# A Mamba and mixture-of-experts layer on one core: new order of its head, new places for its last two chunks

## What is computed

```python
h = _layernorm(x) * (1 + ca) + sa
u = conv1d_depthwise(h, conv_w, taps=4) + conv_b
x_dbl = u @ xproj_w.T                       # dt (128), B (16), C (16)
delta = softplus(dt @ dtproj_w.T + dtproj_b)
h_t = exp(delta * A) * h_{t-1} + delta * B * u      # 16 states per channel
y = sum_n(h * C) + u * D_skip
x = x + ga * y
h = _layernorm(x) * (1 + cb) + sb
logits = tanh(h @ Wg1.T) @ Wg2.T; scores = softmax of the top 2 of 8
x = x + gb * sum_e(scores_e * (silu(h @ Wup_e.T + bup_e) @ Wdown_e.T + bdown_e))
```

## Time and profile before

| | |
|---|---|
| median of three runs | 1440.03 us |
| profiled execution | 1442.15 us |
| its span | 1440.4 us |
| PE busy | 1337.2 us (93%), 7512 instructions |
| DVE busy | 1258.5 us (87%) |
| POOL busy | 1140.5 us (79%) |
| ACT busy | 985.7 us (68%) |
| mean granted PE clock | 0.971 |
| DMA | 160.91 MB, mean 112 GB/s |

### The profile page before, as it was taken

The page is one execution under the profiler, slowest core; times in us unless marked ns, Lnnn a source line. Parts: engine busy times, 40 slices in busy tenths (PEclk is TensorE's granted clock), DMA queues, the critical chain, the costliest instruction groups (busy, mean ns, idle before and its releaser), DMA issues. The chain is left out here.

```text
span 1440.4 us, 23450 instructions
## 1 busy us (share of the span) xinstructions
PE 1337.2 (93%) x7512; PEld 964.4 (67%) x7512; DVE 1258.5 (87%) x1782; ACT 985.7 (68%) x2056; POOL 1140.5 (79%) x1157
## 2 busy tenths in 40 slices
PE   8788768999999999999999999999999999979898
PEld 4456545667766775667667776677676666667687
DVE  4799999899998999899988999899979999795475
ACT  3875786578848785579748885679758765655464
POOL 1699889699997989798988999798979888752243
PEclk9899877999999999999999999999999999999999
DMA  5441112235342434434333424243343343322342
GB/s 196 168 148 60 59 37 87 97 98 157 111 126 78 158 95 117 126 111 130 111 118 100 165 87 137 85 147 118 102 129 93 118 117 117 95 78 70 105 128 91
DMA packets 99250, 160.91 MB, mean 112 GB/s; under 512 B 9245, under 2 KB 33949, under 8 KB 99129
## 3 DMA queue, kind: packets, MB, share of 16 engines
q1 hardware_dynamic: 99128, 159.42, 35.8%
HBM read 150.60 MB, written 8.79 MB: 111 GB/s over the span
## 5 line engine op out<-in xcount | busy, mean ns | idle before, releaser
L785 POOL TENSOR_TENSOR DB<-DU,BR 128x512 f32<-128x512 f32 x448 | 575.6, 1299 | 44.7 <-DVE DU L1177 22.2
L1218 DVE SCALAR_TENSOR_TENSOR ACC<-pb,CTM,ACC 128x512 f32<-128x512 f32 x512 | 374.4, 731 | 52.0 <-PE pb L1419 51.7
L983 ACT ACTIVATE pb<-DELP,AN 128x512 f32<-128x512 f32 x448 | 307.3, 687 | 142.1 <-DVE H L1193 141.4
L1498 PE MATMUL pb<-WD,G 128*128 128x512 f32 x832 | 393.6, 593 | 0.0
L1419 PEld LDWEIGHTS pb<-ID,H 128*128 128x128 f32 x2048 | 245.8, 144 | 157.6 <-issue 89.9
L1419 PE MATMUL pb<-ID,H 128*128 128x128 f32 x2048 | 317.4, 281 | 34.2 <-DVE ACC L1218 29.2
L808 POOL TENSOR_TENSOR G<-TY 128x256 f32<-128x256 f32 x256 | 199.5, 780 | 182.1 <-DVE TY L1274 136.3
L1468 PE MATMUL pb<-H2H,WUH 128*128 128x256 f32 x1024 | 316.6, 309 | 23.0 <-DVE TY L1274 23.0
L1193 DVE TENSOR_TENSOR_SCAN H<-pb,DB 128x512 f32<-128x512 f32 x256 | 309.5, 1210 | 15.1 <-ACT pb L983 13.0
L1470 PE MATMUL pb<-H2H,WUL 128*128 128x256 f32 x1024 | 292.1, 285 | 0.0
L1469 PE MATMUL pb<-H2L,WUH 128*128 128x256 f32 x1024 | 291.8, 285 | 0.0
(11 more groups left out here) (200 smaller groups left out, 1739.4 us busy)
## 6 DMA issues: line engine op xcount, KB each, us to landing
WD<-in_wdT SPq DMA_DIRECT2D x128, 512.0 KB, 5.0
BR<-bscr SPq DMA_DIRECT2D x112, 256.0 KB, 3.9
SR<-sscr SPq DMA_DIRECT2D x128, 128.0 KB, 4.4
DU<-in_x SPq DMA_DIRECT2D x8, 1024.0 KB, 6.7
ACC<-in_x SPq DMA_DIRECT2D x16, 512.0 KB, 3.9
out<-ACC SPq DMA_DIRECT2D x32, 256.0 KB, 2.1
BR<-bscr SPq DMA_DIRECT2D x32, 128.0 KB, 3.3
DU<-in_xpT SPq DMA_DIRECT2D x8, 320.0 KB, 3.2
```

The lines of the kernel that those rows point to most:

```text
L785: eng.tensor_tensor(DB[:, i % NDB], DU[:, c % 2, r], BR[:, n % 2], ALU.mult).then_inc(S["dbu"], 1)
L983: eng.activation(DA[i % NDA][:], DEL[:, c % 2, r], ACT.Exp, scale=AN[:, r, n:n + 1]).then_inc(S["da"], 1)
L1218: eng.scalar_tensor_tensor(out=acc, in0=banks[bank_of["flip", c, n, r]][:], scalar=1.0 if n < 0 else CTM[:, c % 2, j, st:st + 1], in1=acc, ...
L1498: eng.matmul(DN[j][:], G[:, (cs * NM + m) % NG, j * 128:j * 128 + 128], WD[:, (cs * NE + m // 2) % NWD, m % 2], start=False, stop=m == NM ...
```

## The change

In the head: the tap order goes tile by tile (three taps of tile 0, then of tile 1, with tiles 2 and 3 mixed); `decay` moves behind the taps; `diag` moves from the place just after the first scan to ahead of the statistics, and now waits for its own inputs; `gbcp` moves behind the first `da`; the weights of row group 0 are loaded in two halves with a semaphore each, and the product waits for the second half in its middle. In chunk 1's table the statistics (`sta`, `nma`, `stb`) get later places. For chunks 6 and 7 the tables FAST, TAIL, FAST_PAIRS, TAIL_PAIRS, LOW and three of ROUTER get new numbers, and the split of the down products starts at pair (13,3) and not (13,0). The diff, cut:

```diff
 ATTENTION1 = {
-    "ldx": -11, "sta": (2, 2, 7, 8), "nma": 6, "stb": (11, 11, 14, 22), "rsa": 23, "pad": 36,
+    "ldx": -11, "sta": (5, 6, 8, 10), "nma": 11, "stb": (12, 12, 15, 22), "rsa": 23, "pad": 36,
...
-HEAD_TAPS = ((0, 2), (0, 1), (1, 2), (0, 0), (2, 2), (1, 1), (3, 2), (2, 1), (1, 0), (3, 1), (2, 0), (3, 0))
+HEAD_TAPS = ((0, 2), (0, 1), (0, 0), (1, 2), (1, 1), (1, 0), (2, 2), (2, 1), (3, 2), (2, 0), (3, 1), (3, 0))
...
-TAIL = {"sr": -1, "wd": 1, "up": (-3, -2), "th": (4, 4), "ys": (7, 7), "t1": (4, 7), "g": (7, 7), "dn": (16, 16),
-        "to": (18, 18), "fin": (16, 25), "out": (20, 34), "gbl": 17, "xa": 34}
+TAIL = {"sr": -9, "wd": -11, "up": (-2, -1), "th": (3, 3), "ys": (6, 7), "t1": (4, 5), "g": (7, 7), "dn": (1, 14),
+        "to": (16, 19), "fin": (18, 21), "out": (12, 29), "gbl": -4, "xa": 37}
...
-FAST_PAIRS = [51, 58, 64, 72, 77, 82, 86, 96, 101, 108, 112, 117, 122, 127, 133, 138]
-TAIL_PAIRS = [69, 74, 86, 91, 118, 126, 130, 135, 143, 149, 157, 166, 169, 179, 186, 196]
+FAST_PAIRS = [51, 58, 64, 70, 76, 82, 87, 92, 99, 106, 111, 116, 123, 131, 142, 156]
+TAIL_PAIRS = [71, 85, 100, 109, 120, 134, 138, 144, 150, 156, 165, 180, 185, 195, 202, 211]
...
-SPLIT_FROM = (13, 0)
-LOW = {"wh": (5, 5), "wl": 11, "gh": (7, 8), "gl": (11, 12), "dn": (14, 16)}
+SPLIT_FROM = (13, 3)
+LOW = {"wh": (5, 5), "wl": 8, "gh": (9, 10), "gl": (9, 12), "dn": (18, 18)}
...
-FIRST = ((1, ("diag",)), (4, ("gbt",)), (4, ("gbm",)), (8, ("gbb",)), (10, ("gbe",)), (11, ("rowz", 4)),
+FIRST = ((4, ("gbt",)), (4, ("gbm",)), (8, ("gbb",)), (10, ("gbe",)), (11, ("rowz", 4)),
...
-    a = [("begin",), ("warm", -1, WARM["begin"])] + [("sta", 0, j) for j in range(4)] + [("rsa", 0)] + [("xn", 0, j) for j in range(4)]
-    a += [("pad", 0), ("decay",), ("rows", 1), ("rcp", 1), ("rows", 0), ("rcp", 0), ("tr", 0, 0), ("rt", 1), ("mod", 1)]
+    a = [("begin",), ("warm", -1, WARM["begin"]), ("diag",)] + [("sta", 0, j) for j in range(4)] + [("rsa", 0)] + [("xn", 0, j) for j in range(4)]
+    a += [("pad", 0), ("rows", 1), ("rcp", 1), ("rows", 0), ("rcp", 0), ("tr", 0, 0), ("rt", 1), ("mod", 1)]
...
-    a += [("warm", -2, WARM["proj"])]
+    a += [("decay",), ("warm", -2, WARM["proj"])]
...
-                    eng.dma_start(WM[0], wm_v[0]).then_inc(S["d_wm0"], 16)
+                    eng.dma_start(WM[0][:, 0:2], wm_v[0][:, 0:2]).then_inc(S["d_wm0"], 16)
+                    eng.dma_start(WM[0][:, 2:4], wm_v[0][:, 2:4]).then_inc(S["d_wmh"], 16)
...
                     for kk in range(4 if what == "rows" else 1):
+                        if g == 0 and kk == 2:
+                            eng.wait_ge(S["d_wmh"], 16)
```

More of the change, by code:

```diff
@@ L71 @@
              "r52": 104, "sw": 104},
-    "final": {"fst": (17, 18), "nmf": 20, "fsu": (22, 22), "frs": 23, "fxn": (35, 37), "ftr": (44, 49),
-             "fev": (47, 49), "hh": 58, "hl": (59, 71), "r1": 79, "r12": 81, "r2": 85, "r22": 88, "r3": 91,
-             "r31": 93, "e1": 94, "r4": 93, "r40": 95, "r41": 95, "r42": 96, "sel1": 95, "sel2": 97, "r5": 96,
-             "r52": 101, "sw": 101},
-    "last": {"fst": (16, 19), "nmf": 27, "fsu": (25, 25), "frs": 27, "fxn": (35, 39), "ftr": (46, 49),
-             "fev": (47, 50), "hh": 52, "hl": (52, 58), "r1": 54, "r12": 56, "r2": 60, "r22": 60, "r3": 64,
-             "r31": 64, "e1": 64, "r4": 67, "r40": 67, "r41": 69, "r42": 72, "sel1": 70, "sel2": 73, "r5": 77,
-             "r52": 76, "sw": 77},
@@ L80 @@
-    "split": {"fst": (-43, -39), "nmf": -42, "fsu": (-39, -39), "frs": -38, "fxn": (-35, -33), "ftr": (-35, -29),
-             "fev": (-31, -27), "hh": -25, "hl": (-25, -24), "r1": -26, "r12": -20, "r2": -20, "r22": -20, "r3": -19,
-             "r31": -18, "e1": -17, "r4": -18, "r40": -15, "r41": -15, "r42": -15, "sel1": -14, "sel2": -12,
-             "r5": -11, "r52": -10, "sw": -4}}
+    "final": {"fst": (17, 22), "nmf": 26, "fsu": (24, 24), "frs": 26, "fxn": (36, 38), "ftr": (43, 45),
+             "fev": (46, 49), "hh": 58, "hl": (57, 70), "r1": 81, "r12": 86, "r2": 89, "r22": 84, "r3": 96,
+             "r31": 96, "e1": 97, "r4": 98, "r40": 100, "r41": 100, "r42": 100, "sel1": 103, "sel2": 103, "r5": 107,
+             "r52": 106, "sw": 106},
@@ new lines @@
+    "last": {"fst": (14, 19), "nmf": 27, "fsu": (25, 25), "frs": 31, "fxn": (36, 43), "ftr": (46, 51),
+             "fev": (47, 50), "hh": 55, "hl": (52, 60), "r1": 55, "r12": 56, "r2": 60, "r22": 61, "r3": 66,
+             "r31": 66, "e1": 67, "r4": 69, "r40": 69, "r41": 71, "r42": 74, "sel1": 70, "sel2": 76, "r5": 79,
+             "r52": 79, "sw": 79},
+    "split": {"fst": (-46, -43), "nmf": -44, "fsu": (-39, -39), "frs": -38, "fxn": (-38, -36), "ftr": (-35, -29),
+             "fev": (-34, -30), "hh": -23, "hl": (-25, -22), "r1": -24, "r12": -23, "r2": -20, "r22": -20, "r3": -19,
+             "r31": -18, "e1": -16, "r4": -17, "r40": -15, "r41": -15, "r42": -14, "sel1": -14, "sel2": -14,
+             "r5": -9, "r52": -10, "sw": -8}}
@@ L88 @@
 PAIR = {"sr": 0, "wd": 1, "up": (0, 2), "th": (4, 4), "ys": (6, 6), "t1": (4, 6), "g": (7, 9), "dn": (12, 14),
         "to": (18, 18), "fin": (21, 26), "out": (20, 28), "gbl": 22, "xa": 29}
-FAST = {"sr": -4, "wd": -5, "up": (0, 2), "th": (3, 3), "ys": (4, 4), "t1": (5, 5), "g": (4, 7), "dn": (10, 13),
-        "to": (14, 19), "fin": (20, 26), "out": (31, 34), "gbl": 21, "xa": 11}
-TAIL = {"sr": -1, "wd": 1, "up": (-3, -2), "th": (4, 4), "ys": (7, 7), "t1": (4, 7), "g": (7, 7), "dn": (16, 16),
-        "to": (18, 18), "fin": (16, 25), "out": (20, 34), "gbl": 17, "xa": 34}
+FAST = {"sr": -5, "wd": -3, "up": (0, 2), "th": (3, 3), "ys": (4, 4), "t1": (3, 3), "g": (4, 6), "dn": (10, 13),
+        "to": (14, 14), "fin": (19, 27), "out": (35, 35), "gbl": 21, "xa": 21}
@@ L839, in _ @@
                 elif what == "diag":
+                    eng.wait_ge(S["d_pv"], 16)
+                    eng.wait_ge(S["id"], 1)
                     for dt in sorted(pe_tiles(1)):
```

6 lines of the change are left out of this document (3 added, 3 removed).

## The result

| | before | changed |
|---|---|---|
| median | 1440.26 us (4 runs, 1439.8 to 1442.7) | 1420.57 us (4 runs, 1418.3 to 1423.3) |
| ratio | | 0.9861, 95% interval 0.9839 to 0.9882 |
| span of the profiled execution | 1440.4 us | 1421.5 us |
| PE busy | 1337.2 us (93%) | 1335.9 us (94%) |
| DVE busy | 1258.5 us (87%) | 1251.3 us (88%) |

The change gained 19.7 us; the forecast was 9.6, its range ended at 1421. The table shows at once that the two halves of the sum went wrong in opposite directions: the head's gain was there at 90 us and gone at 131, and the last two chunks gave everything.

The account below looks back on a forecast made before the run. The prediction took a dependent chain to bound the head, DVE chunk 7's scans, and PE the time after the last scan. Gains of 3.3 + 3.3 + 3.0 = 9.6 us took 1440.03 to 1430.4 us; range 1421 to 1438.

Parts of the forecast that it names:

- 0.96 + 0.57: Head: 0.96 us from taps tile by tile, 0.57 us from the gate row's copy moved behind the first factor block.
- Halves: Head: loading row group 0's weights in two halves gains 0, since PE never waited for that load.
- Diagonals: Head, ACT: diagonal copies (2.4 us in all) moved before the normalisation are hidden in ACT's wait there, costing 0.
- The stalls of chunk 0: Chunk 0: DVE's 2.32 us wait and POOL's 3.04 us wait ease; 1.8 us gained, bounds 0 to 2.32.
- Rival B: Head's gain is lost in chunk 0 to POOL and the weight loads; only the tail gains, 1433.7 us; chance 0.10.
- DVE's relief: Chunk 7 before the last scan: fewer weight and G differences save DVE 5.2 us, less 1.9 of extra PE work.
- The wait of 5.00: After the last scan: PE's wait for a late score row goes; with its low clock 8.0 us to be had.
- The new waits: After the last scan: 2.2 us at half-chunk 15's transposes, 1.1 at the second up products, 1.7 lost to low clock.
- (a): Half-chunk 15's transposes: ACT needs some 5.0 us, PE has 2.8 of work meanwhile, so 2.2 us of new wait.
- C: Better than summed: DVE's relief spares PE its waits and both low-clock spells, 3.9 + 6 + 6, 1424 us; chance 0.12.
- A: Under the scans PE becomes the bound, as slower products eat DVE's relief: 4.4 us gained, 1435.6 us; chance 0.17.
- D: Tail: score rows come late behind weight loads, 8.0 us per event; two events make it slower, 1446 us; chance 0.08.

Follow-up runs that it names:

- e20_change_again: The changed kernel, unchanged, run again on the same chip as two other kernels: 1419.87 us, ratio to before 0.9866 (0.9849 to 0.9884).

## Why the prediction was wrong, step by step

**The head: 3.3 forecast, nothing arrived.** The steps up to the first scan were right. From PE's first product on row group 0 to the first scan it was 32.89 us (46.48 - 13.59), and is 31.47: 1.42, against 0.96 + 0.57 = 1.53. Halves: PE's first product on them is at 12.96 to 13.52 in the new head's traces and at 13.26 to 13.59 in the four without halves: 0, as forecast. Diagonals: PV landed at 6.9, the copies ran from 6.91 to 9.36, the normalisation began at 12.14: hidden. The stalls of chunk 0, 1.8 in the sum, were priced too high: between the first scan (1.97 us earlier) and scan 20 (3.07 earlier) the two traces gain 1.1, and over four traces of the old head and sixteen of the new scan 20 is at 89.5 against 87.4, 2.1 in all. DVE's waits of 0.77 and 2.32 us up to 64 us became 0.77, 1.53 and 0.16, only 0.6 less. At scan 40 the old head's traces stand at 130.1 to 132.1 and those of the new one, with the old taps, at 130.9 to 131.4 (129.28 in the one whose tap wasn't held). The step that failed is "Chunks 1 to 5 keep their order and pass the shift on": before them, still in chunk 0, stood a tap whose length depends on how it falls among POOL's products. Rival B had this outcome, at 0.10; it named POOL, but not a DVE operation held beside it.

**The rule.** I had set the Trainium skill's rule (page "SBUF — State Buffer", section "SBUF: two separate sides": a vector operation with two SBUF inputs and a GpSimd (POOL) one that reads SBUF can't share a port pair: whichever starts first has it for its whole instruction) against the weight differences only, where it changed 2 us. The traces agree with it in that the two operations that it would have warned of are the held ones, with two SBUF operands each, 6.11 and 3.58 us, and that the second took 0.2 us once its second operand was a scalar per partition. They go beyond it in the size: by the rule the vector operation waits for one GpSimd instruction; here four more products of POOL began before the tap had its turn, and two more before the difference.

**Under the scans: 3.3 forecast, 4.7 measured** (119.4 to 114.7; 8.3 in e20_change_again, without the held operation). The 5.2 us of DVE's relief were sized about right: one weight difference and one of G are left before the last scan, as forecast, DVE's busy time in the stretch fell by 6.7 us in e20_change_again (4.1 with the held operation), and three weight differences and six of G put back cost 5 to 6. The failing step is the one after it, "PE waited 6.4 us for DVE's gated products in these 45 us, so it has the room". PE's idle time under the scans is no room. All of PE's work must be done by the end, and after the last scan PE is the bound, so from chunk 7 on an idle microsecond of PE comes back at the end as a longer time. PE's idle time under the scans fell from 10.9 to 3.5 us, and PE did 2.7 us more of its work there (at full speed 109.5 against 106.8) and 2.0 less after them. This is an account of the traces and not an experiment of its own. The view I took, DVE the bound until the last scan, then PE, made me price only what reached the last scan. The term that I subtracted, 1.9 for unsplit products, is 0.7 in PE's work by the traces.

**After the last scan: 3.0 forecast, 13.8 measured** (137.9 to 124.2). The wait of 5.00 went, and with it the low clock; its price of 8.0 lies between the 5.7 and the 10.5 that two experiments give. The new waits were overpriced: at the transposes 1.5 instead of 2.2, at the second pair none instead of 1.1 (0.4 at the router's product beside it), and no low clock instead of 1.7. The sum of (a) was off too: its items add to 5.2 and not 5.0. The step that failed most is what the sum left out between the last scan and the wait of 5.00: 1.9 us for a gated product right after the last scan, 3.4 us at 1.2 GHz behind it (1.7 lost), and 1.1 for a low part of G at 1321.8. "From there to the end PE is full in both orders: 0" failed as well, by 2.0: PE was all but full there in the changed kernel only, and before it stood for low parts of G from 1358 on:

```profile
1350.00:1360.00 10.00, 9.46 (x55) 8.15 (x55) 7.42 (x27) 6.02 (x15) 2.24 (x4) 1.00 0.01 2
1360.00:1380.00 20.00, 19.50 (x131) 17.70 (x131) 10.36 (x15) 9.51 (x25) 6.74 (x6) 1.00 0.44 133
```

Of the 13.8 us, 7.0 are idle time, 4.8 clock, and 2.0 work that PE had done before. That all this went because ACT and DVE were no longer behind is argued; what the runs show is that 12.1 of it come back as a loss when the score rows and weights of chunk 7 go late again.

**Rivals.** C named this mechanism (PE spared its waits and both spells of low clock), with 12 us for it where 18.5 came, and with a head that did not. A is refuted: PE's waits under the scans fell, none took their place. D's event, a wait of DVE of over 3 us for a score row, does not occur in the changed kernel; its only such wait after the last scan is 0.5 us. The range ended 0.4 us above the result: it took in C's middle, not what C's mechanism could give at most.
